# The gate of a finished item stands one step later in VectorE's order

## The reference

```python
xi, z = split(x @ in_proj_w.T)
xc = silu(conv4(xi) + conv_b)
dt_r, B, C = split(xc @ x_proj_w.T)
dt = softplus(dt_r @ dt_proj_w.T + dt_proj_b)
h = exp(dt * A) * h + (dt * xc) * B      # over 4096 positions, for each of the 16 states
y = sum over states of (h * C) + xc * D
out = (y * silu(z)) @ out_proj_w.T       # y * silu(z) is "the gate"
```

## Time and profile before

| what | before |
|---|---|
| median of 3 runs | 17287.28 us (17285.9 to 17292.63) |
| profiled execution, its time | 17281.15 us |
| profiled execution, its span | 17279.2 us |
| VectorE busy | 14988.9 us (87%) |
| GpSimd busy | 14970.7 us (87%) |
| TensorE busy | 14535.6 us (84%) |
| ScalarE busy | 11261.9 us (65%) |

### The profile page before, as it was taken

One profiled execution on the slowest core, in us unless ns is written; L12 is line 12 of the kernel. 1 busy time (PEld: TensorE's weight loads), 2 busy tenths in 40 slices (PEclk: granted clock), 3 DMA queues, 4 the chain that ended last, 5 costly groups with the idle time before them and its releaser, 6 DMA issues. The chain is left out here.

```text
span 17279.2 us, 159098 instructions
## 1 busy us (share of the span) xinstructions
PE 14535.6 (84%) x30720; PEld 5796.6 (34%) x30720; DVE 14988.9 (87%) x13132; ACT 11261.9 (65%) x18548; POOL 14970.7 (87%) x6268
## 2 busy tenths in 40 slices
PE   6888878888788887888878888788887888878888
PEld 2333333333333333333333333333333333333333
DVE  7999969999699996999969999699996999869998
ACT  4667657676566765667656666566665666656675
POOL 5999969999699996999969999699986999869998
PEclk8999989999899998999989999899998999989999
DMA  3444434444344443444434444344443444434443
GB/s 130 155 156 160 156 108 156 154 159 157 111 154 156 158 154 115 155 154 158 152 116 157 152 157 156 114 154 156 156 154 118 157 153 154 151 118 152 152 152 135
DMA packets 739059, 2535.91 MB, mean 147 GB/s; under 512 B 77240, under 2 KB 78016, under 8 KB 721728
## 3 DMA queue, kind: packets, MB, share of 16 engines
q1 hardware_dynamic: 738112, 2527.45, 42.8%
HBM read 2376.15 MB, written 150.99 MB: 146 GB/s over the span
## 5 line engine op out<-in xcount | busy, mean ns | idle before, releaser
L1200 POOL TENSOR_TENSOR RING<-RING,CS 128x1024 f32<-128x1024 f32 x4096 | 9832.9, 2419 | 1054.6 <-DVE RING L921 1037.3
L921 DVE TENSOR_TENSOR_SCAN RING<-DA,HS,RING 128x512 f32<-128x512 f32 x8192 | 9948.9, 1264 | 785.1 <-ACT DA L649 528.7
L369 PE MATMUL YP<-RING,EYE 128*128 128x512 f32 x16384 | 8378.6, 643 | 1931.3 <-POOL RING L1200 1899.3
L649 ACT ACTIVATE DA<-ITEM,AN 128x512 f32<-128x512 f32 x8192 | 5526.7, 685 | 3369.3 <-DVE RING L921 3359.7
L369 PEld LDWEIGHTS YP<-RING,EYE 128*128 128x128 f32 x16384 | 3122.7, 199 | 6731.5 <-issue 3495.4
L901 DVE TENSOR_TENSOR RING<-DTP,BS 128x1024 f32<-128x1024 f32 x2816 | 3374.9, 1206 | 0.2 <-DMA BS<-bc_rows 0.2
L1187 POOL TENSOR_TENSOR RING<-ITEM,BS 128x1024 f32<-128x1024 f32 x1280 | 3019.4, 2360 | 8.6
L369 PE MATMUL FL<-XN,WC 128*128 128x512 f32 x4096 | 1954.3, 622 | 48.1 <-ACT XN L734 36.6
L1205 POOL TENSOR_TENSOR ITEM<-ITEM,EX 128x1024 f32<-128x1024 f32 x256 | 602.6, 2354 | 1048.7 <-ACT EX L703 1048.7
L369 PEld LDWEIGHTS FL<-XN,WC 128*128 128x128 f32 x4096 | 847.4, 207 | 1194.5 <-issue 1151.3
L662 ACT ACTIVATE ITEM<-FL,COL 128x512 f32<-128x512 f32 x512 | 347.9, 680 | 1202.1 <-PE FL L369 1202.1
(11 more groups left out here) (122 smaller groups left out, 10420.8 us busy)
## 6 DMA issues: line engine op xcount, KB each, us to landing
BS<-bc_rows SPq DMA_DIRECT2D x2048, 512.0 KB, 4.9
CS<-bc_rows SPq DMA_DIRECT2D x2048, 512.0 KB, 3.6
XR<-in_x SPq DMA_DIRECT2D x128, 1024.0 KB, 7.4
x_slices<-XR SPq DMA_DIRECT2D x64, 1024.0 KB, 8.0
XR<-x_slices SPq DMA_DIRECT2D x64, 1024.0 KB, 7.4
out<-XR SPq DMA_DIRECT2D x64, 1024.0 KB, 7.9
ITEM<-in_wqkv SPq DMA_DIRECT2D x24, 1024.0 KB, 5.5
bc_rows<-ROWS SPq DMA_DIRECT2D x256, 64.0 KB, 4.5
```

The lines of the kernel that those rows point to most:

```text
L369: return pe.matmul(*a, **k)
L649: act.activation(DA[:, h, :], DT[:, i % 2, h, :], ACT.Exp, scale=AN[:, h, s:s + 1]).then_inc(dA_ready, 1)
L921: dve.tensor_tensor_scan(H[:, slot(n), h, :], DA[:, h, :], U[:, slot(n), h, :], HS[:, i % ITEMS, h, s:s + 1], ALU.mult, ALU.add).then_inc( ...
L1200: pool.tensor_tensor(G[:, slot(n)], H[:, slot(n)], CS[:, s % C_ROWS, :].unsqueeze(1).broadcast_to([P, NH, T]), ALU.mult).then_inc(g_ready, 1)
```

## The change

The gate of item w-1 is issued behind scan 3 of item w instead of behind scan 2; with j = 3 behind scan 4 instead of behind scan 3. No other stream is touched, and no instruction is added or removed. The gate behind the last item of an image (`last_end`) stays.

```diff
                     n = w * NS + s
                     make_ahead(tile, n, j, first=first)
                     scan(tile, n, first=first)
-                    if s == 2 + d and not first:
+                    if s == 3 + d and not first:
                         gate(tile, w - 1)
                     if s == 6 + d and not first:
                         add_skip(tile, w - 1)
```

## The result

The changed kernel takes 17929.76 us (median of 4 runs, 17919.92 to 17932.08) against 17286.89 us for the kernel before in the same series: ratio 1.037, 95% interval 1.0352 to 1.0388, so 643 us slower. The forecast was 17795 us, 508 slower, in a range of 17600 to 17980. The profiled execution has a span of 17926.6 us and a mean granted clock of 0.916 for TensorE; before, they were 17279.2 us and 0.931.

The account below looks back on a forecast made before the run. Bound: GpSimd's fixed stretch plus VectorE's path from scan 2 to scan 10. Terms for j = 0 to 3, 62 + 19 + 45 + 381 = 507 us on 17281, plus 6 for the median, gave 17795 us, range 17600 to 17980.

Parts of the forecast that it names:

- The bound: Per item: GpSimd's fixed stretch plus VectorE's path from scan 2 to scan 10, with the gate on that path.
- j = 0, 1, 2, the silus: Silus behind the later gate delay scan 4's factor: +1.1, +0.3 and +0.7 us an item.
- the term for `dt_proj`: With j = 0, TensorE, late by the gate, delays the split of dt and factors of steps 7 and 8: 0.4 us.
- j = 3, z behind the sum: On TensorE z waits behind the sum of step 0, which waits for the gate: scan 5 +6.8 us.
- The load without a drain: ScalarE's table load between silu and factor takes 1.28 us, without the skill's added drain of 1.38.
- Window 31: An image's last window, without silus or z: its gate moves at no cost, under 1 us an image.
- Only the silus count: Rival: TensorE's order does no harm; j = 3 costs +2.0 at scan 5, 17525 us in all; chance 0.10.
- The wait simply goes: Rival: the gate's wait on VectorE vanishes and the kernel is faster, 16900 us; chance 0.05.
- Hidden: Rival: GpSimd is the only bound, so the time stays within 0.2%; chance 0.07.
- Worse: Rival: with j = 3 TensorE stays at the lower clock, late before `dt_proj`; above 18040 us; chance 0.12.

Follow-up runs that it names:

- e3: The changed kernel with, at j = 3 on TensorE, the two matmuls of z ahead of the sum of step 0: 17756.0 us, ratio 1.0274.
- e5: Against the kernel before, gate and silus both one step later with j = 0 and 1 alone: 17427.2 us, ratio 1.0079.

## Why the prediction was right

*The bound.* Right. GpSimd's idle rose with VectorE's, and VectorE had no pause behind the new wait with j = 3: 38.00 of 38.00.

*j = 0, 1, 2, the silus.* Right in mechanism, low in size: 1.1, 0.3, 0.7 forecast, 1.7, 1.0, 0.9 measured. With j = 0 and 1 this lies above the terms' own ranges (up to 1.5 and 0.8); the total is in its range because that adds up the worst of all four kinds. The wait ahead of scan 4 is 2.85 to 2.91, "about 3". Two parts were too small. First, the term for `dt_proj` stood at 0.4 for j = 0 and 0 for j = 1. In the mean the idle ahead of scans 7 and 8 is 0.35 and 0.16 with j = 0, and ahead of 7, 8 and 10 it is 0.42, 0.19 and 0.34 with j = 1: 0.5 and 0.95. The prediction said that TensorE has no pause there in which to make up for the late gate. It has one now, 1.6 to 2.0 of waiting for the gate, and what comes with it in 50 of 120 windows is the lower clock: scans 7 and 8 wait only where the sum of step 0 ran partly at it. The prediction counted the clock with j = 3 alone. Second, with j = 0 scan 3 waits 0.78 for its factor, 0.5 more than in the run with j = 3 set back: TensorE's xi is later behind a long item with j = 3. The run with j = 3 alone puts this at 47 us, 0.8 for each item with j = 0, and the run with j = 3 set back takes j = 0 down to 1.0. I had treated the four kinds as independent.

*j = 3, z behind the sum.* Right: +7.2 against +6.8. The parts: TensorE idle 6.87 (forecast 6.9); sum and z 6.43, where I took 5.7 between 5.2 and 6.42, so the row of eight matmuls behind a wait of 6.10 was the one to take (the 3.35 for four slow ones is in no row; the trace after has 3.57 from start to start); idle ahead of scan 5 9.5 in the mean (near 9). The gate ends 6.6 us later into the item in the mean, not 7.0, which hides part of the 0.7 by which sum and z were taken too small. The run with z first takes 5.4 off scan 5, and the run with the filled wait shows 2.2 of it to be the clock. By the kernel with the lower clock after every wait in the Trainium skill ("TensorE: Matmul & The Clock Gate", HAM oscillation) the term was the larger one, and the trace agrees, with a granted clock of 0.57 behind the wait against the 1.00 of the run with the wait filled.

*The load without a drain.* The trace after agrees with that of before and not with the Trainium skill ("ScalarE: Activation LUTs", "What ACT_TABLE_LOAD costs"): the load at 5446.94 takes 1.28, and the factor starts at 5448.23.

*Window 31.* I gave it under 1 us an image, its gate at no cost. That was wrong: from its scan 0 to the end of its scan 15 it takes 60.7 us in the mean instead of 58.7, 2.0 of the 2.8 an image. TensorE has no front to do there, waits 9.14 for the gate, and the output projection comes late for the skip, as VectorE's timeline shows:

```profile
2222.12 0.69 DVE L933 TENSOR_TENSOR YB<-YB,FL 128x512 f32<-128x512 f32 x1 [1.99 <-PE FL L369]
```

*Rivals.* "Only the silus count" (17525) fell with e3. "The wait simply goes" (16900) fell: with nothing but the gate of j = 0, 1, 2 moved, it is 138 us slower. Its mechanism did occur in e5, where the factor of step 4 was free of the gate, and was worth 0.6 and 1.8 at scan 5; the second path took it back. "Hidden" fell with both. "Worse" named the right neighbour, TensorE's lateness ahead of `dt_proj`, and the lower clock as its cause, but for j = 3, where scans 7 and 8 don't wait at all in the changed kernel; it came with j = 0 and 1, and small.

*What stays open.* Why the stretches at the lower clock with j = 0 fall onto xi more often behind a longer item: no run sets it apart. And whether j = 0 and 1 with the later gate could be made faster than before with TensorE's short wait for the gate filled, or with less for it to do: the orders tried did not do it, and no run fills that wait or joins z first with a filled one. No run beat the kernel before.

## What to carry to other kernels

An engine's wait that the profile shows large may be the cheapest place for it. Before an instruction is moved later, list all who wait for its semaphore and, for each, what stands behind that wait in its queue; the price is set by the one with the least cover, here 1.1 us of U against 4.0 of silus, and z queued behind a sum that didn't concern it. When an engine is late, reordering its queue can just choose which consumer waits (four of the six orders here gained 16 us or nothing; z first and then dt first, with j = 3, gained 174 and 83 us): look at all its consumers' waits, not only at the one that was cured. For TensorE look at its granted clock behind each new wait as well. Here, behind new waits of 1.6 to 2.0 us, the sum was slow in 50 of 120 windows (2.8 to 3.7 us instead of 1.98), and in these scans 7 and 8 waited 1.53.

## What was unexpected

Five more matmuls in a wait made the kernel 121 us faster, with TensorE's clock at 1.00 instead of 0.57 behind it. And a window can cost time in its neighbour: with the edit in j = 3 alone, 47 us of 476 arose with j = 0, where the eight matmuls of xi took 4.29 us in the mean instead of 3.86, and in one window shown here 4.63 at a granted clock of 0.72.
